# Scores of half the TensorE array over 62 and 64 rows in place of 33 and 35, in a two-layer transformer on one core

## The reference

```
w = einsum('bhnd,bhmd->bhnm', q, k) * rsqrt(8)
w = softmax(w)                       # layer 0 masks it first
attn = einsum('bhnm,bhmd->bhnd', w, v)
```

## Time and profile before

| | |
|---|---|
| median of the two runs shown | 2974.7 us |
| profiled execution, span | 2986.01 us, 2984.3 us |
| PE busy with matmuls | 2604.5 us (87%) |
| PE busy with weight loads | 1428.2 us (48%) |
| DVE, ACT, POOL busy | 1631.8 (55%), 1394.6 (47%), 857.2 us (29%) |
| granted TensorE clock, mean over the span | 0.729 |
| layer 0 attention, routing, experts, layer 1 | about 48 to 1155, 1155 to 1400, 1400 to 1670, 1720 to 2984 us |

### The profile page before, as it was taken

One profiled execution on the slowest core, in us unless ns is written; L12 is line 12 of the kernel. 1 busy time (PEld: TensorE's weight loads), 2 busy tenths in 40 slices (PEclk: granted clock), 3 DMA queues, 4 the chain that ended last, 5 costly groups with the idle time before them and its releaser, 6 DMA issues. The chain is left out here.

```text
span 2984.3 us, 46587 instructions
## 1 busy us (share of the span) xinstructions
PE 2604.5 (87%) x14818; PEld 1428.2 (48%) x14818; DVE 1631.8 (55%) x4330; ACT 1394.6 (47%) x3057; POOL 857.2 (29%) x1296
## 2 busy tenths in 40 slices
PE   3999999999999996444999489999999999999995
PEld 1455555555555553344999333344444444444443
DVE  3554664554465433543222157677777777777753
ACT  0343553443354342001444137566666666666662
POOL 3111111111111001773000434444444444443212
PEclk9955875765585555555999758678778777877786
DMA  4111111111111100112544221111111111111100
GB/s 142 59 56 44 59 47 44 55 57 44 43 61 47 44 2 19 41 44 84 142 142 143 72 73 62 51 54 55 54 54 56 54 53 54 56 54 49 48 5 11
DMA packets 143330, 174.24 MB, mean 58 GB/s; under 512 B 33704, under 2 KB 96880, under 8 KB 142960
## 3 DMA queue, kind: packets, MB, share of 16 engines
q1 hardware_dynamic: 133440, 153.86, 16.6%
q0 software_dynamic: 8192, 16.79, 1.9%
q10 hardware_dynamic: 1456, 0.60, 0.1%
HBM read 111.39 MB, written 57.67 MB: 57 GB/s over the span
## 5 line engine op out<-in xcount | busy, mean ns | idle before, releaser
L2078 DVE TENSOR_REDUCE l_rowmax<-pair 128x2 f32<-128x1024 f32 x512 | 618.0, 1221 | 246.1 <-PE pair L1842 226.0
L1987 ACT ACTIVATE l_probs<-bank 128x512 f32<-128x512 f32 x1024 | 550.1, 604 | 238.8 <-PE bank L1853 233.6
L704 DVE CUSTOM_DVE_ANT_0 pair<-pair,mask_rows_q 128x512 f32<-128x512 f32 (+3 forms) x1024 | 477.2, 519 | 335.7 <-PE pair L518 335.6
L518 PE MATMUL pair<-k_stack,q_stack 33*128 33x512 f32 (+3 forms) x1024 | 383.4, 545 | 31.3 <-DMA k_stack<-scratch 19.7
L1853 PE MATMUL bank<-q_stack,k_stack 35*128 35x512 f32 x1024 | 382.7, 573 | 21.0 <-ACT l_probs L1987 18.1
L622 ACT ACTIVATE l_probs<-bank 128x384 f32<-128x384 f32 (+3 forms) x672 | 276.4, 437 | 224.4 <-PE pair L536 121.1
L1864 PE MATMUL bank<-l_probs,v_aug 128*32 128x512 f32 x2048 | 352.7, 768 | 13.2 <-ACT l_probs L1987 11.8
L1842 PE MATMUL pair<-k_stack,q_stack 33*128 33x512 f32 x1024 | 310.5, 506 | 58.8 <-DVE l_rowmax L2078 36.7
L1853 PEld LDWEIGHTS bank<-q_stack,k_stack 35*128 35x128 f32 x1024 | 152.4, 218 | 385.4 <-ACT l_probs L1987 202.9
L531 PE MATMUL bank<-q_stack,k_stack 35*128 35x384 f32 (+3 forms) x672 | 302.3, 532 | 9.1 <-ACT l_probs L622 9.1
L550 PE MATMUL bank<-l_probs,v_aug 128*32 128x512 f32 (+3 forms) x2048 | 289.6, 652 | 4.2 <-ACT l_oT L662 2.0
(11 more groups left out here) (275 smaller groups left out, 3782.3 us busy)
## 6 DMA issues: line engine op xcount, KB each, us to landing
q_stack<-scratch SPq DMA_DIRECT2D x512, 64.0 KB
k_stack<-scratch SPq DMA_DIRECT2D x512, 64.0 KB
experts_w<-in_w SPq DMA_DIRECT2D x72, 256.0 KB, 2.5
scratch<-l_q_parts SPq DMA_DIRECT2D x32, 512.0 KB, 2.8
scratch<-l_k_parts SPq DMA_DIRECT2D x32, 512.0 KB, 3.7
experts_rows<-rows_in SPq DMA_DIRECT2D x72, 128.0 KB, 2.1
rows_out<-experts_y SPq DMA_DIRECT2D x72, 128.0 KB, 2.1
q_stack<-l_rowmaxT SPq DMA_DIRECT2D x512, 4.0 KB
```

The costliest lines, as they stand in the source:

```text
L518: nc.tensor.matmul(bank[:, 0:keys(t)], q[:, t * P:(t + 1) * P], k[:, 0:keys(t)], start=True, stop=True).then_inc(s_mm, 1)
L704: nc.vector.tensor_tensor_reduce(scores, scores, m["mask_rows_q"][:, S - keys(t):S], 1.0, LOWEST, ALU.add, ALU.max, rowmax[:, g % 2, c:c + ...
L1987: nc.scalar.activation(probs[:, (a * HG + j) % PSLOTS, :], bank[:, :], ACT.Exp, scale=SCALE).then_inc(t_read, 1)
L2078: nc.vector.tensor_reduce(largest, pair[:, :].rearrange("p (i k) -> p i k", i=2), X_AXIS, ALU.max).then_inc(s_read, 1)
```

## The change

The number of rows over which the scores are contracted, and with it the place of the two rows of maxima. The maxima move from rows 33 and 34 of each half to rows 62 and 63, its last two. The max scores run over rows 0 to 61 in place of 0 to 32, the exp scores over rows 0 to 63 in place of 0 to 34. Rows 32 to 61 of q hold the zeros of `load_constants`, so the sums are the same. Columns, banks, waits, and the number, size and order of all instructions and transfers on every engine are as before; the two 4 KB rows that each pair of `stack_max` transfers writes go to other partitions.

```diff
@@ -40,8 +40,7 @@
 PARTS = 2
 HALF = P // 2
 SLAB = PARTS * D
-ZEROROW = PARTS * SLAB
-MAXROW = ZEROROW + 1
+MAXROW = HALF - PARTS
 STACK_DMAS = 8
@@ -514,7 +513,7 @@ scores_for_max, layer 0
-                q, k = (stacked_rows(stacks[n % 2], j, g, ZEROROW + 1) for stacks in (q_stack, k_stack))
+                q, k = (stacked_rows(stacks[n % 2], j, g, MAXROW) for stacks in (q_stack, k_stack))
                 nc.tensor.matmul(bank[:, 0:keys(t)], q[:, t * P:(t + 1) * P], k[:, 0:keys(t)], start=True, stop=True).then_inc(s_mm, 1)
@@ -527,7 +526,7 @@ scores_for_exp, layer 0
-                    q, k = (stacked_rows(stacks[n % 2], j, g, MAXROW + PARTS) for stacks in (q_stack, k_stack))
+                    q, k = (stacked_rows(stacks[n % 2], j, g, HALF) for stacks in (q_stack, k_stack))
                     nc.tensor.matmul(banks[-1][:, first(t):S], k[:, t * P:(t + 1) * P], q[:, first(t):S], start=True, stop=False)
@@ -1838,7 +1837,7 @@ scores_for_max, layer 1
-                q, k = (stacked_rows(stacks[b % 2], j, g, ZEROROW + 1) for stacks in (q_stack, k_stack))
+                q, k = (stacked_rows(stacks[b % 2], j, g, MAXROW) for stacks in (q_stack, k_stack))
@@ -1849,7 +1848,7 @@ scores_for_exp, layer 1
-                q, k = (stacked_rows(stacks[b % 2], j, g, MAXROW + PARTS) for stacks in (q_stack, k_stack))
+                q, k = (stacked_rows(stacks[b % 2], j, g, HALF) for stacks in (q_stack, k_stack))
```

## The result

The changed kernel took 2647.02 and 2661.38 us in two runs, a median of **2654.2 us** against 2974.7 us: a ratio of 0.8923, with a 95% interval of 0.8805 to 0.904. The forecast was 2585 us, with a range of 2530 to 2665 us: faster, as forecast, and at the upper end of the range. The profiled execution took 2661.38 us (span 2659.6 us), 325 us less than the one of before; the forecast was 390.

The account below looks back on a forecast made before the run. PE was taken to bound both attention stages, held at half the clock by scores over few rows. Savings of 238 + 17 + 135 = 390 us off 2986 gave 2596, or 2585 us against the median; range 2530 to 2665.

Parts of the forecast that it names:

- What holds the clock: Both attention stages: the clock goes by how much of the array works, rows included; mean clock about 0.9 after.
- Rival A: Whole kernel: rows don't count for the clock, or zeros don't, so nothing changes, 2975 us; chance 0.10.
- The price of the full clock in layer 0: Layer 0's loop: 0.778 us per max score at full clock against 1.16 at half, 258 us less at most.
- How much of layer 0 stays at half the clock: Layer 0: 4 us a batch and a few at the start, some 60 us, cost 20, leaving a 238 us gain.
- The last batch of layer 0: Layer 0's last batch, 55 us at 0.53 without max scores: comes in at full clock and saves 17 us.
- Layer 1: Second attention stage: a third off its time at half the clock, 5 us a batch left there; saves 135 us.
- Nothing for the rest of the edit: Score matmuls, stack filling and transfers: more rows contracted cost no time; 63 us at most, taken as nothing.
- rival B: Score matmuls: clock stays and time grows with rows, 15 ns each, 3038 us, 2.1% slower; chance 0.02.
- Rival C: Attention stages: clock rises less often, from light quads or DVE starving PE; half the gain, 2780 us; chance 0.05.

Follow-up runs that it names:

- group 3: Last set of follow-up kernels, most adding edits to the change, compared with the same runs of the kernel before, median 2966.17 us.
- all three: The change plus earlier q and k projections, layer 0's last batch filled with unread max scores, and wider max scores in its light quads: 2535.11 us, 0.8561.

## Why the prediction was right, and where it was off

**What holds the clock** (right, now shown). I read that the clock goes by how much of the array is at work, rows included. The rows of the scores alone moved it, in steps with their number; 64 unread score matmuls took the last batch from 0.52 to 1.00 while PE was busy for less of it (0.91 against 0.94); fillers moved it a little; zeros count like any work. Rival A falls in each of its forms: busy time, columns, halves, zeros. The Trainium skill (TensorE: Matmul & The Clock Gate, Part 1: The HAM clock gate) lets activity release the throttle. By that rule, read as time busy, layer 0 would have been at the high level before the change. The traces agree with it only where activity means cells at work: PE was 26.70 of 26.70 us busy at 0.50 in the changed kernel too. What exactly is counted stays open: if it were cells alone, 29 rows on the max scores should bring what 29 on the exp scores bring, and they bring 75 us against 128.

**The price of the full clock in layer 0** (right). 0.778 us for each L518 and 49.8 us a batch were forecast; 0.781 and 50.0 came. PE's share is 0.91 (forecast 0.92) and DVE's 0.71 (0.7).

**How much of layer 0 stays at half the clock** (mis-sized, the largest miss). I left 4 us a batch and some at the start, 60 us in all. It was 133 us by the record and 13 at the start that the record misses, 146 us, which at a third cost 49 us in place of 20: 29 more. The waits for k_stack, 11.2 us where before there were 4.2, are 7 more. 206 came in place of 242 (238 were forecast from 954 of these batches' 960 max scores), and these two terms are the 36. I had foreseen the light quads. I had not seen that the stacks' transfers would be late in batches of 50 us, though I had looked for waits: I took the 0.778 us from stretches in which no batch of before began late. Nor had I seen how long a fall can last: 26.7 us at half the clock behind a wait of 1.38 us. In other batches 6.8 us followed the same kind of wait, so I can't say what sets the length.

**The last batch of layer 0** (wrong, 17 forecast, -1 measured). I let it come in at full clock and keep it. It came in so, but lost the clock 2 us later, at 893.6. It has no max scores, so too little is at work even with 64 rows: 0.52 as before. The kernel with unread scores shows that this was the cause, and that the batch was worth 16 us: 58.8 to 42.3.

**Layer 1** (right in kind, 135 forecast, 122 measured). A batch took 68.2 us, not 65 to 67. PE waits for the maxima for 2.34 us at one place, and with the maxima halved a batch took 3.3 us less. The earlier trace rows had warned of this: DVE 10.16 of 10.30 us. I used that row to choose the ratio and left 5 us a batch at half the clock for DVE's long operations, but not the waits themselves. DVE is no floor for a whole batch, since it is busy for 54 of 68.2 us, but it is one in stretches. The short falls of the clock (0.97) have a part too: in group 3 the same rows gave batches of 64.9 us without one, as forecast. How the 3 us divide is open.

**Nothing for the rest of the edit** (right). Score matmuls take 0.46 to 0.49 us at full clock with 33, 35, 62 and 64 rows, and the loop passes a max score in 0.781 us in place of 0.778, so rival B's price is nil. By the same Trainium skill page (LDWEIGHTS) a weight load takes its time by its columns; no run here times one by itself at both numbers of rows. Routing and experts moved by 2 us.

**Rival C** (a part only) named the two ways in which the gain was cut, light quads and waits that cost a longer fall. It took half of the gain for them; they took 65 of 390 us, by all terms together.

## What to carry to other kernels

Put the granted clock beside PE's busy row before anything else. Where PE is always busy at half the clock, count the cells that its matmuls use, and if rows or columns are free, fill them: addressing memory that holds zeros was enough here, and it cost nothing, with the streamed columns, the halves of the array in use and the number of matmuls as they were. A mean of the clock needs a look at durations first, since its record can start late, here by up to 250 us. Then look for the places that drop the clock, waits of a microsecond or narrow tiles, and cure all of them together: here the kernels with one or two of the cures kept at most 21 of the 63 us that all three gave layer 0.

## What the runs showed of the hardware

- Rows contracted count for the clock within a half of the array: layer 0's clock was 0.62 with 33 and 35 rows, 0.71 with 47 and 49, 0.83 and 0.88 with 62 and 64, the gap in the record counted at half. Operands that are zero on both sides count like others.
- Doing more can take less time: 64 unread matmuls shortened a batch from 58.8 to 42.3 us.
- The record of the clock says 1.00 until the clock first rises, though durations are those of 0.50: until 136 us before, 102 in the change, 250 and 235 in two other kernels.
- Waits of about a microsecond can drop the clock, and the fall can outlast them by far: 26.7 us behind a wait of 1.38 us, 23.9 behind 0.89, but 6.8 behind 1.29 and 2.51. Light quads alone bring 13.7 us in a batch.
- A filler over the whole array, 512 columns, cost about 0.3 us in the loop at full clock and 0.7 at half, an estimate from batch times.
- Open: why 29 more rows bring 128 us in layer 0 on the exp scores and 75 on the max scores, what sets the length of a fall, and why layer 1 was 40 us shorter and nearly without falls in group 3.
